# An attention kernel's scan moved to the next step, its hiding to GpSimd, and its narrow counts from ScalarE to VectorE

## The chip, the cores and the metric

The kernel runs on one core of a Trainium2 chip. The metric is the device time of one execution in microseconds (us), the median of three runs. Engines are called by the short names of the profile: PE is TensorE, ACT is ScalarE, DVE is VectorE, POOL is GpSimd, SP issues the transfers.

## The reference

For 16 batches of 512 tokens with 128 channels: `x = x + layernorm(attention(layernorm(x)))`, and then `x = x + layernorm(ffn(layernorm(x)))`. The feed-forward part is gated by silu, with 384 hidden channels. The attention has 16 heads; what matters here is this part of it (shapes for one batch and 16 heads):

```python
dots = jnp.einsum('bhid,bhjd->bhij', q, k) * scale      # 512 x (16 memory + 512) scores
dots = jnp.einsum('bhij,hk->bkij', dots, pre_proj)
dots = jnp.where(causal[None, None], neg, dots)
top = lax.top_k(dots, 64)[0]
vk = top[..., -1:]                                      # the 64th largest of each row
dots = jnp.where(dots < vk, neg, dots)
attn = jax.nn.softmax(dots, axis=-1)
attn = jnp.einsum('bhij,hk->bkij', attn, post_proj)
out = jnp.einsum('bhij,bhjd->bhid', attn, v)
```

## The kernel before

The mixing matrices are folded into the weights ahead of the loop. Then one "step" is one head of one batch; a batch has 16 steps. The 512 rows of a head stand as four tiles of 128 rows. By causality the tiles have 528, 400, 272 and 144 columns (keys and 16 memory columns), 1344 in all. Each engine has its own queue of instructions in the order of the program, and the engines meet at semaphores; `g` is the number of the step over all batches, `s` the step within a batch. The Python branch `lagged(kind, s, lag)` says whether the head that entered `lag` steps ago is worked on in this step.

The 64th largest score of each row is found by guessing a threshold. For a head that entered k+1 steps ago, ACT counts guess k (k = 0, 1, 2): a Sign activation over each tile with the guess as bias, summed by the accumulator (L871). From the counts DVE makes the next guesses with a chain of small instructions on 12 or 24 columns (L1123 to L1149), called the update here; the last of them raises `guess_ready`. After three guesses (LAG_K = 4) DVE counts with the fourth guess and keeps the 0/1 marks in `work` (L1014, "found"), takes the marked scores out of the way (L1080, the hide), scans what is left for its 8 largest (L1092, MAX8, four tiles), and picks the right one of nine by rank (L1099) and value (L1107). POOL computes the rank offsets from the count (L1260). DVE also checks whether the count was near enough (L1078 spread, L1084 missed); PE sums that over the rows (L761, the "FLAG" use of the shared misc banks), ACT copies the sum to `flags` (which raises `misc_free`), and DVE loads it into a register in the next step (L1029). Where it isn't zero an exact search runs, which is rare.

One step later (LAG_P = 5) DVE applies the threshold to the exponentials that ACT made (L1048, four tiles, called the applies) and takes a reciprocal of the sums (L1053). POOL scales by it (L1269) and copies the memory columns out (L1276, pmem). PE transposes the result in three groups (L737), ACT copies each group (L882, probsT), and PE multiplies it into the y bank (L724). In the same step DVE evicts the new head's scores from PSUM (L1061), with its maxima. Layer norms are done by DVE (statistics) and POOL (L1194 to L1210) in certain steps, and the feed-forward part goes through PE, ACT, POOL (L1307) and DVE (L1165) in steps 9 to 14.

The order of DVE in a step before: found, applies, reciprocal, eviction, spread, hide, missed, update, scans, rank, value. The order of ACT: counts of guesses 2 and 1, a copy from misc, the copy for the next head, counts of guess 0, a copy, then probsT copies and exponentials mixed, the flags copy, the last probsT copy. The order of POOL: negated maxima, seed of a guess, offset, scaling, pmem, the memory columns of the new head, extras (norms, gate product). ACT's counts wait for the update of the step before:

```python
at_least(act, first_ready if k == 0 else guess_ready, g if k == 0 else g - 1)
```

and DVE waits for the flags with

```python
dve.wait_ge(misc_free, flag_index(kind, b, s) + 1)   # the FLAG use of step s - 1
```

Of the kernel before, what the change touches and what calls it, by code (L numbers as in the profile page):

```python
# [31 lines left out]
P = 128  # L32
# [9 lines left out]
MASKED = -2.0 ** 100  # L42
# [10 lines left out]
RING = 8  # L53
# [3 lines left out]
LAG_P = 5  # L57
LAG_V = 6
# [18 lines left out]
          4: [("U", 7), ("U", 8)],  # L77
          5: [("PM", 0), ("PM", 1)],
          6: [("U", 9), None],
          7: [("MEM", 0), ("MEM", 1)],  # L80
          8: [("U", 10), ("X1T",)],
          9: [("GATE", 0), ("UP", 0)],
          10: [("GATE", 1), ("UP", 1)],
          11: [("GATE", 2), ("UP", 2)],
          12: [("U", 11), ("U", 12)],
          13: [("DOWN", 0), ("DOWN", 1)],
          14: [("U", 13), ("U", 14)],
          15: [("U", 15), None]}
# [15 lines left out]
def guess_table():  # L104
# [23 lines left out]
    for t in range(T):  # L128
        for i in range(P):
            n = P * t + i + 1  # L130
            z = quantile(min(max((AIM - 0.4 * M) / n, 0.02), 0.97))
            density = n * pdf(z) + M * pdf(z / 4.4) / 4.4
            active = n + M > TOPK
            table[i, t] = z
            table[i, T + t] = z - FAR / (2 * density)
            table[i, 5 * T + 9 * T + t] = float(active)
            table[i, 5 * T + 10 * T + t] = 0.0 if active else -FMAX
        for k in range(GUESSES):
            table[:, 2 * T + k * T + t] = ROW[t] - 2 * AIM - 0.25
        table[:, 5 * T + 9 * t:5 * T + 9 * t + 9] = np.arange(9) - TOPK  # L140
# [8 lines left out]
def flagged(kind, s):  # L149

    return lagged(kind, s, LAG_K)
# [120 lines left out]
def build(nc, table, x, wq, wk, wv, pre, post, memk, memv, wo, bo, wgate, wup, wdown, out):  # L272
    with ExitStack() as ctx:  # L273
# [12 lines left out]
        work = sb("work", [P, WIDE])  # L286
# [37 lines left out]
        onesP = sb("onesP", [P, P])  # L324
        signs = sb("signs", [P, GUESSES, ROW[T - 1]], mybir.dt.int8)
        found = sb("found", [P, T])
# [18 lines left out]
        minus_one = sb("minus_one", [P, T])  # L345
# [72 lines left out]
        found_ready = sem("found_ready")  # L418
        offset_ready = sem("offset_ready")
        select_step = sem("select_step")  # L420
# [140 lines left out]
        def _(pe):  # L561
# [179 lines left out]
            def batch(kind, b, par):  # L741
                def step(s):
# [12 lines left out]
                    if lagged(kind, s, LAG_P):  # L755
                        turn(head_of(s, LAG_P), g - LAG_P, 0)
                        turn(head_of(s, LAG_P), g - LAG_P, 1)
                    if flagged(kind, s):
                        pe.wait_ge(bad_ready, g - LAG_K + 1)
# [3 lines left out]
                    if lagged(kind, s, LAG_P):  # L763
                        turn(head_of(s, LAG_P), g - LAG_P, 2)
# [9 lines left out]
        def _(act):  # L774
# [20 lines left out]
            for q in range(4):  # L795
                nc.scalar.mul(a_all[:, 4 * q:4 * q + 4, :], banks[q][:, :].rearrange("p (h n) -> p h n", h=4),
                              DH ** -0.5).then_inc(a_taken, 1)
            nc.scalar.mul(amem[:, :, :], banks[4][:, 0:H * M].rearrange("p (h n) -> p h n", h=H),
                          DH ** -0.5).then_inc(a_taken, 1)
# [29 lines left out]
            def batch(kind, b, par):  # L829
                def step(s):  # L830
# [30 lines left out]
                    def count(k):  # L861
# [23 lines left out]
                    def exponentials(p):  # L885

                        if lagged(kind, s, LAG_K):
                            ge, t = g - LAG_K, ORDER[p]
# [3 lines left out]
                            nc.scalar.activation(row(expo, ring(head_of(s, LAG_K), ERING), t),  # L892
                                                 row(scores, ring(head_of(s, LAG_K), RING), t), ACT.Exp,
                                                 bias=negmax[:, bass.ds(ring(head_of(s, LAG_K), RING), 1), t]
# [31 lines left out]
        def _(dve):  # L926
# [4 lines left out]
            nc.vector.memset(minus_one[:, :], -1.0).then_inc(consts_made, 1)  # L931
# [35 lines left out]
            nc.vector.tensor_tensor(a_sq[:, :, :], a_all[:, :, :], a_all[:, :, :], ALU.mult).then_inc(squared, 1)  # L967
# [32 lines left out]
            dve.wait_ge(state_set, 3)  # L1000
            nc.vector.tensor_copy(offset[:, :, 9:10].squeeze(2), cap)

            def batch(kind, b, par):
                def step(s):
                    g = b * H + s
                    v = nc.vector
                    slot_k, slot_p = ring(head_of(s, LAG_K), RING), ring(head_of(s, LAG_P), RING)
                    gk, gp = g - LAG_K, g - LAG_P
                    selects, applies = lagged(kind, s, LAG_K), lagged(kind, s, LAG_P)
                    moves = any(lagged(kind, s, k + 1) for k in range(GUESSES))  # L1010
                    now, soon, past = s % STATES, (s + 1) % STATES, (s - 1) % STATES

                    def count_found(t):
                        v.tensor_scalar(work[:, AT[t]:AT[t] + ROW[t]], row(scores, slot_k, t), guessed[:, t:t + 1],  # L1014
                                        None, ALU.is_ge, ALU.add, accum_out=found[:, t:t + 1]).then_inc(found_ready, 1)

                    if selects:
# [6 lines left out]
                        count_found(ORDER[1])  # L1024
                    if applies:

                        dve.wait_ge(misc_free, flag_index(kind, b, s) + 1)
                        alone(dve)
                        rows_missed = dve.value_load(flags[0:1, T:T + 1].bitcast(I32), min_val=0, max_val=2 ** 31 - 1)  # L1029
                    if selects:  # L1030
                        count_found(ORDER[2])
                        count_found(ORDER[3])
                    if applies:

# [19 lines left out]

                    if kind != "drain":
# [9 lines left out]
                    if s == 6 and kind != "first":  # L1065
                        dve.wait_ge(y_taken, b)
                        norm_stats(kind, b, "Y", ybuf)
                    if s == 7 and kind != "first":
# [3 lines left out]
                    if s == 14 and kind != "first":  # L1072
# [3 lines left out]
                    if selects:  # L1076
                        dve.wait_ge(found_ready, 4 * gk + 4)
                        v.scalar_tensor_tensor(out=spread[:, :], in0=found[:, :], scalar=-2.0 * AIM, in1=found[:, :],  # L1078
                                               op0=ALU.add, op1=ALU.mult).then_inc(select_step, 1)
# [3 lines left out]
                        dve.wait_ge(select_step, 1)  # L1083
                        v.scalar_tensor_tensor(out=missed[:, 0:T], in0=spread[:, :], scalar=WINDOW ** 2 + 0.5 - AIM ** 2,  # L1084
                                               in1=active, op0=ALU.is_gt, op1=ALU.mult,
                                               accum_out=missed[:, T:T + 1]).then_inc(bad_ready, 1)

                    def top_scan():
                        if selects:
                            dve.wait_ge(select_step, 2)  # L1090
                            for t in ORDER:
                                v.max(candidates(now)[:, t, 1:9], work[:, AT[t]:AT[t] + ROW[t]]).then_inc(select_step, 1)  # L1092

                    def pick_rank():

                        if selects:
# [249 lines left out]
```

## Time and profile before

| what | value |
|---|---|
| median of three runs | 3636.93 us (3633.64 to 3641.19) |
| the profiled execution: its time | 3636.07 us |
| the profiled execution: its span | 3634.3 us |
| DVE busy | 3292.4 us, 91% of the span |
| ACT busy | 3199.3 us, 88% |
| PE busy | 2795.9 us, 77% |
| POOL busy | 1551.4 us, 43% |

The span runs from the first to the last instruction. Shares are averages over the whole span; what a change is worth is read from one step's order. A row of a timeline has the start in us from the span's start, the duration in us, engine, line, operation, output and input; where an engine stood still before it, the wait and what ended it stand in brackets. Neighbouring DVE or ACT instructions overlap by a little, so a cost in a row of instructions is the distance of starts, not the duration.

### The profile page before, as it was taken

To read this page: it belongs to the slowest core of one execution; us is meant where nothing else is said; L and a number is where in the kernel's file an instruction comes from. 1 tells how busy PE (TensorE), PEld (TensorE's weight loads), DVE (VectorE), ACT (ScalarE), POOL (GpSimd) and SP (SyncE) were. 2 spreads that over 40 slices of the span, in tenths; PEclk is the share of its full clock that TensorE was granted. 3 is DMA by queue.
4 is the path that set the end of the run, shared out by engine and by line. 5 is a ranking of instruction groups with operands and counts; after the bars stand their busy time and mean duration, and the time that the engine had idled before them with its cause. 6 is when DMAs were issued, how large, how long until landed. Compare 5 with 4: busy or idle time off the path is not lost. (4 is left out here: it accounts for less than half of the span.)

```text
span 3634.3 us, 67348 instructions
## 1 busy us (share of the span) xinstructions
PE 2795.9 (77%) x13751; PEld 1808.7 (50%) x13751; DVE 3292.4 (91%) x12492; ACT 3199.3 (88%) x9018; POOL 1551.4 (43%) x2663
## 2 busy tenths in 40 slices
PE   7777778777777878778778867877777788877765
PEld 3455455545545545555455545544555455545544
DVE  4699999999999999999999999999999999999994
ACT  1799999999979999999999979998999999999973
POOL 3233444444434444444444444443444444444433
PEclk9888999988888899888998888899889998899886
DMA  1000000000000000000000000000000000000000
GB/s 41 7 2 2 5 8 5 8 2 5 8 4 8 5 8 2 5 8 5 8 5 7 2 4 8 5 8 2 5 8 5 8 5 8 2 5 8 2 7 4
DMA packets 31375, 22.37 MB, mean 6 GB/s; under 512 B 3201, under 2 KB 30338, under 8 KB 30722
## 3 DMA queue, kind: packets, MB, share of 16 engines
q1 hardware_dynamic: 30722, 16.03, 1.6%
q14 instruction: 532, 4.36, 0.4%
q8 instruction: 121, 1.98, 0.2%
HBM read 11.83 MB, written 4.19 MB: 4 GB/s over the span
## 5 line engine op out<-in xcount | busy, mean ns | idle before, releaser
L871 ACT ACTIVATE signs<-scores,state 128x528 int8<-128x528 f32 (+3 forms) x3072 | 1764.3, 574 | 181.8 <-DVE state L1149 103.4
L713 PE MATMUL s_bank<-xn,gT 128*128 128x512 f32 (+3 forms) x2048 | 900.6, 568 | 1.7 <-issue 0.7
L1269 POOL TENSOR_SCALAR probs<-probs,rinv 128x528 f32<-128x528 f32 (+3 forms) x1024 | 547.1, 553 | 507.3 <-DVE rinv L1053 507.3
L737 PE MATMUL t_bank<-ident,probs 128*128 128x128 f32 x2560 | 482.7, 313 | 299.1 <-POOL probs L1269 289.7
L724 PEld LDWEIGHTS y_bank<-u_all,probsT 128*128 128x128 f32 x5120 | 619.9, 194 | 133.4 <-issue 124.2
L724 PE MATMUL y_bank<-u_all,probsT 128*128 128x128 f32 x5120 | 625.2, 278 | 7.1 <-ACT probsT L882 7.1
L1260 POOL TENSOR_TENSOR offset<-consts,found 128x36 f32<-128x36 f32 x256 | 161.7, 632 | 1047.5 <-DVE work L1014 1047.5
L871 ACT ACTIVATION_READ_ACCUMULATOR signs<-scores,state 128x1 f32 x3072 | 575.7, 187 | 0.0
L737 PEld LDWEIGHTS t_bank<-ident,probs 128*128 128x128 f32 x2560 | 299.7, 153 | 506.8 <-issue 398.6
L1048 DVE SCALAR_TENSOR_TENSOR probs<-scores,kth,expo 128x528 f32<-128x528 f32 (+3 forms) x1024 | 522.8, 565 | 24.8 <-issue 19.1
L892 ACT ACTIVATE expo<-scores,negmax 128x528 f32<-128x528 f32 (+3 forms) x1024 | 535.0, 575 | 0.0
L1014 DVE TENSOR_SCALAR_CACHE_REDUCE work<-scores,state 128x528 f32<-128x528 f32 (+3 forms) x1024 | 515.5, 559 | 20.2 <-issue 12.3
L1061 DVE TENSOR_SCALAR_CACHE_REDUCE scores<-s_bank,memmax 128x512 f32<-128x512 f32 (+3 forms) x1024 | 502.5, 547 | 3.8 <-PE s_bank L715 3.4
L713 PEld LDWEIGHTS s_bank<-xn,gT 128*128 128x128 f32 x2048 | 393.4, 239 | 222.4 <-issue 212.3
L882 ACT COPY probsT<-t_bank 128x512 f32<-128x512 f32 (+1 forms) x768 | 390.6, 509 | 104.5 <-PE t_bank L737 102.7
L1092 DVE MAX8 state<-work 128x8 f32<-128x528 f32 (+3 forms) x1024 | 444.9, 500 | 0.0
L1080 DVE SCALAR_TENSOR_TENSOR work<-work,scores 128x1344 f32<-128x1344 f32 x256 | 404.9, 1582 | 0.0
L599 PE MATMUL misc<-b_all,xn 128*128 128x512 f32 x512 | 281.3, 631 | 50.5 <-ACT u_all L803 46.3
L1276 POOL COPY pmem<-probs 128x64 f32<-128x64 f32 x256 | 303.5, 1186 | 35.9 <-issue 2.5
L761 PE MATMUL misc<-missed,onesP 128*1 128x5 f32 x512 | 49.4, 168 | 343.0 <-DVE missed L1084 340.0
L634 PE MATMUL misc<-xn,a_all 128*128 128x512 f32 x512 | 263.2, 596 | 0.0
L715 PE MATMUL s_bank<-causal,ident 128*128 128x128 bf16 x1024 | 250.5, 245 | 0.0
(148 smaller groups left out, 3384.9 us busy)
## 6 DMA issues: line engine op xcount, KB each, us to landing
xwork<-in_L_attn_x_dram SPq DMA_DIRECT2D x17, 256.0 KB, 2.8
xres<-in_L_attn_x_dram SPq DMA_DIRECT2D x16, 256.0 KB, 2.9
out_dram<-ybuf SPq DMA_DIRECT2D x16, 256.0 KB, 2.4
u_all<-in_L_attn_Wq_dram SPq DMA_DIRECT2D x1, 512.0 KB, 3.7
u_all<-in_L_attn_Wk_dram SPq DMA_DIRECT2D x1, 512.0 KB, 4.5
u_all<-in_L_attn_Wv_dram SPq DMA_DIRECT2D x1, 512.0 KB, 5.3
u_all<-in_L_attn_Wo_dram SPq DMA_DIRECT2D x1, 512.0 KB
expo<-in_L_ffn_w_gate_dram SPq DMA_DIRECT2D x1, 192.0 KB, 4.7
```

The lines of the kernel that those rows point to most:

```text
L713: nc.tensor.matmul(score_part(t, 0, KEYS[t]), lhsT=gT[s % 2][:, t * P:(t + 1) * P], rhs=xn[par][:, 0:KEYS[t]], start=True, stop=False, ski ...
L724: mm = nc.tensor.matmul(y_bank[:, t * P:(t + 1) * P], lhsT=probsT[:, h % 2, at:at + P], rhs=u_all[:, j, h * D:(h + 1) * D], start=False, s ...
L737: mm = nc.tensor.transpose(t_bank[q % 2][:, at:at + P], probs[:, h % 2, KEY_AT[t] + j * P:KEY_AT[t] + (j + 1) * P], ident[:, :])
L871: nc.scalar.activation(signs[:, k, 0:ROW[t]], row(scores, ring(head_of(s, k + 1), RING), t), ACT.Sign, bias=guesses(s % STATES, k, GUESSES ...
L882: nc.scalar.copy(probsT[:, h % 2, PART_AT[q]:PART_AT[q + 1]], t_bank[q % 2][:, 0:PART_AT[q + 1] - PART_AT[q]]).then_inc(t_taken, 1)
L892: nc.scalar.activation(row(expo, ring(head_of(s, LAG_K), ERING), t), row(scores, ring(head_of(s, LAG_K), RING), t), ACT.Exp, bias=negmax[: ...
L1014: v.tensor_scalar(work[:, AT[t]:AT[t] + ROW[t]], row(scores, slot_k, t), guessed[:, t:t + 1], None, ALU.is_ge, ALU.add, accum_out=found[:, ...
L1048: v.scalar_tensor_tensor(out=probs[:, slot_p % 2, AT[t]:AT[t] + ROW[t]], in0=row(scores, slot_p, t), scalar=kth[:, bass.ds(slot_p, 1), t], ...
L1061: v.tensor_scalar(keys(scores, slot, t), score_part(t, 0, KEYS[t]), 1.0, memmax[par][:, t, bass.ds(s, 1)], ALU.mult, ALU.max, accum_out=ro ...
L1080: v.scalar_tensor_tensor(out=work[:, :], in0=work[:, :], scalar=-FMAX, in1=scores[:, bass.ds(slot_k, 1), :].squeeze(1), op0=ALU.mult, op1= ...
L1092: v.max(candidates(now)[:, t, 1:9], work[:, AT[t]:AT[t] + ROW[t]]).then_inc(select_step, 1)
L1269: nc.gpsimd.tensor_scalar(prb, prb, rinv[:, slot_p, t:t + 1], 1.0, ALU.mult, ALU.mult).then_inc(scaled, 1)
```

## The change

1. The scan, rank and value of a head are done one step later and at the start of DVE's step. There are two `work` buffers and two `found` buffers. LAG_P goes from 5 to 6, LAG_V from 6 to 7, and exponentials and flags get a lag of their own, LAG_E = 5. The wait for the flags and their register load stand in front of the third of the four scans.
2. The hide goes from DVE (one instruction, 1344 columns) to POOL (four, one per tile, between its scaling and its pmem copy). Scores are scaled by 2^-60, so that subtracting the 0/1 marks hides a score; MASKED, the guess table and Exp's scale follow.
3. The check (spread, missed) and the update stand behind the value and ahead of found. The update works on the counts of the step before, and writes the guesses for the step that it stands in. Three of the four found counts stand behind the applies.
4. ACT counts three tiles of each guess. DVE counts the 144-wide tile of the three guesses behind the eviction (a compare with accumulation, out to `marks` in bf16), and the update gets one more small instruction for it.
5. POOL's offset and its copy of the memory columns stand at the start of its step; the offset is for the head of LAG_P. ACT's flags copy comes behind the last probsT copy. Extras of PE, the silu product and the norms move by up to one step.

```diff
 LAG_K = 4
-LAG_P = 5
-LAG_V = 6
+LAG_E = 5
+LAG_P = 6
+LAG_V = 7
...
 # ACT, one guess
-                        for p, t in enumerate(ORDER):
+                        for p, t in enumerate(ORDER[:3]):
-                            at_least(act, counted[k], 4 * (g - k - 1) + p)
+                            at_least(act, counted[k], 3 * (g - k - 1) + p)
...
 # ACT, the end of its step
+                    take_turned(2)
                     if flagged(kind, s):
-                        at_least(act, probs_ready, 4 * (g - LAG_K))
+                        at_least(act, probs_ready, 4 * (g - LAG_E))
                         take(kind, b, par, ("FLAG", s), flags[:, :], misc[misc_place(kind, par, ("FLAG", s))][0:1, 0:T + 1])
-                    take_turned(2)
...
 # DVE, the start of its step
+                    if applies:
+                        dve.wait_ge(hidden, 4 * gp + 4)
+                        alone(dve)
+                        for p, t in enumerate(ORDER):
+                            if p == 2:
+                                dve.wait_ge(misc_free, flag_index(kind, b, s) + 1)
+                                alone(dve)
+                                rows_missed = dve.value_load(flags[0:1, T:T + 1].bitcast(I32), min_val=0,
+                                                             max_val=2 ** 31 - 1)
+                            v.max(candidates(past)[:, t, 1:9], work[:, s % 2, AT[t]:AT[t] + ROW[t]]).then_inc(select_step, 1)
+                        dve.wait_ge(offset_ready, gp + 1)
...
 # DVE, behind the rank, the value and the check
+                    if moves:
+                        for k in range(GUESSES):
+                            if lagged(kind, s, k + 2):
+                                dve.wait_ge(counted[k], 3 * (g - k - 1))
+                        guess, other = guesses(last, 0, GUESSES), pair(now, S_OTHER, 1)
+                        dve.wait_ge(narrow_step, sum(lagged(kind, s, k + 2) for k in range(GUESSES)))
+                        dve.sem_clear(narrow_step)
+                        v.scalar_tensor_tensor(out=narrow_miss, in0=narrow[:, :], scalar=-2.0, in1=narrow_aim,
+                                               op0=ALU.mult, op1=ALU.add).then_inc(guess_step, 1)
...
 # DVE, behind the eviction
+                        for k in counts_now:
+                            v.tensor_scalar(marks[:, k], row(scores, ring(head_of(s, k + 1), RING), 0),
+                                            guesses(now, k, GUESSES)[:, 0:1], None, ALU.is_ge, ALU.add,
+                                            accum_out=narrow[:, k:k + 1]).then_inc(narrow_step, 1)
...
-                        v.scalar_tensor_tensor(out=work[:, :], in0=work[:, :], scalar=-FMAX,
-                                               in1=scores[:, bass.ds(slot_k, 1), :].squeeze(1),
-                                               op0=ALU.mult, op1=ALU.add).then_inc(select_step, 1)
...
 # POOL, behind the scaling and ahead of the pmem copy
+                    if lagged(kind, s, LAG_K):
+                        gk, slot_k = g - LAG_K, ring(head_of(s, LAG_K), RING)
+                        for p, t in enumerate(ORDER):
+                            pool.wait_ge(found_ready, 4 * gk + p + 1)
+                            alone(pool)
+                            wrk = work[:, s % 2, AT[t]:AT[t] + ROW[t]]
+                            nc.gpsimd.tensor_tensor(wrk, row(scores, slot_k, t), wrk, ALU.subtract).then_inc(hidden, 1)
```

## Rows read from the trace of the kernel before

**Rows 1.** The page, busy time of each engine

```profile
PE 2795.9 (77%) x13751; PEld 1808.7 (50%) x13751; DVE 3292.4 (91%) x12492; ACT 3199.3 (88%) x9018; POOL 1551.4 (43%) x2663
```

**Rows 2.** Timeline of ACT, the y copies of two neighbouring batches

```profile
1658.25 0.56 ACT L901 COPY ybuf<-y_bank 128x512 f32<-128x512 f32 x1
...
1870.77 0.56 ACT L901 COPY ybuf<-y_bank 128x512 f32<-128x512 f32 x1
```

**Rows 3.** Timeline of DVE over one plain step

```profile
1820.13 0.76 DVE L1014 TENSOR_SCALAR_CACHE_REDUCE work<-scores,state 128x528 f32<-128x528 f32 x1
...
1821.79 0.36 DVE L1014 TENSOR_SCALAR_CACHE_REDUCE work<-scores,state 128x144 f32<-128x144 f32 x1
...
1824.29 0.18 DVE L1053 RECIPROCAL rinv<-rowsum 128x4 f32<-128x4 f32 x1
...
1826.32 0.46 DVE L1078 SCALAR_TENSOR_TENSOR spread<-found 128x4 f32<-128x4 f32 x1
1826.70 1.54 DVE L1080 SCALAR_TENSOR_TENSOR work<-work,scores 128x1344 f32<-128x1344 f32 x1
1828.17 0.19 DVE L1084 SCALAR_TENSOR_TENSOR missed<-spread,consts 128x4 f32<-128x4 f32 x1
...
1828.29 0.25 DVE L1123 TENSOR_TENSOR state<-counts,consts 128x12 f32<-128x12 f32 x1
...
1830.04 0.17 DVE L1149 TENSOR_TENSOR state<-state,move 128x12 f32<-128x12 f32 x1
...
1831.97 0.23 DVE L1099 SCALAR_TENSOR_TENSOR offset<-offset,state 128x36 f32<-128x36 f32 x1
...
1832.63 0.76 DVE L1014 TENSOR_SCALAR_CACHE_REDUCE work<-scores,state 128x528 f32<-128x528 f32 x1
```

**Rows 4.** Timeline of ACT over the same step

```profile
1817.50 0.73 ACT L871 ACTIVATE signs<-scores,state 128x528 int8<-128x528 f32 x1 [0.48 <-DVE state L1149]
...
1819.12 0.52 ACT L871 ACTIVATE signs<-scores,state 128x272 int8<-128x272 f32 x1
...
1819.76 0.41 ACT L871 ACTIVATE signs<-scores,state 128x144 int8<-128x144 f32 x1
...
1820.18 0.72 ACT L871 ACTIVATE signs<-scores,state 128x528 int8<-128x528 f32 x1
...
1829.79 0.36 ACT L882 COPY probsT<-t_bank 128x256 f32<-128x256 f32 x1
```

**Rows 5.** Timeline of ACT in the drain, DVE's register load (line L1029), and the apply behind it

```profile
3580.20 0.14 ACT L803 COPY flags<-misc 1x5 f32<-1x5 f32 x1
...
L1029 DVEq TENSOR_LOAD <-flags x1: 303/303/303, 3580.4 to 3580.4; - x1
...
L1029 DVEq SEQ_ASSERT  x1: 23/23/23, 3581.0 to 3581.0; - x1
...
3581.82 0.77 DVE L1048 SCALAR_TENSOR_TENSOR probs<-scores,kth,expo 128x528 f32<-128x528 f32 x1 [3.33 <-issue]
```

**Rows 6.** Groups of DVE by line and shape

```profile
L1092 DVE MAX8 state<-work 128x8 f32<-128x272 f32 x256 | 110.2, 431 | 0.0
...
L1165 DVE SCALAR_TENSOR_TENSOR f_up<-f_tanh,f_up 128x512 f32<-128x512 f32 x48 | 33.1, 690 | 17.4 <-POOL f_up L1307 15.2 <-issue 2.2
```

**Rows 7.** Timeline of POOL; its 512-wide product; lines L1276, L1260 (ns min/median/max)

```profile
1815.82 0.25 POOL L1194 TENSOR_SCALAR vareps<-meanvar 128x4 f32<-128x4 f32 x1
...
1819.58 0.20 POOL L1249 TENSOR_TENSOR negmax<-rowmax,minus_one 128x4 f32<-128x4 f32 x1
...
1824.66 2.11 POOL L1269 TENSOR_SCALAR probs<-probs,rinv 128x528 f32<-128x528 f32 x4 [1.58 <-DVE rinv L1053]
...
L1307 POOL TENSOR_TENSOR f_up<-f_up,f_gate 128x512 f32<-128x512 f32 x48 | 61.6, 1283 | 8.8 <-ACT f_up L803 8.8
...
L1276 POOL COPY pmem<-probs x256: 236/1441/1455, 156.0 to 3586.5; 128x64 f32<-128x64 f32 x128
...
L1260 POOL TENSOR_TENSOR offset<-consts,found x256: 244/671/811, 136.8 to 3572.5; 128x36 f32<-128x36 f32 x128
```

More of the change, by code:

```diff
@@ L1006, in step @@
                     v = nc.vector
[L1007 to L1011, printed above, removed]
-                    def count_found(t):
-                        v.tensor_scalar(work[:, AT[t]:AT[t] + ROW[t]], row(scores, slot_k, t), guessed[:, t:t + 1],
-                                        None, ALU.is_ge, ALU.add, accum_out=found[:, t:t + 1]).then_inc(found_ready, 1)
+                    slot_k, slot_e, slot_p = [ring(head_of(s, lag), RING) for lag in (LAG_K, LAG_E, LAG_P)]
@@ new lines, in step @@
+                    gk, ge, gp = g - LAG_K, g - LAG_E, g - LAG_P
+                    selects, checks, applies = [lagged(kind, s, lag) for lag in (LAG_K, LAG_E, LAG_P)]
+                    moves = any(lagged(kind, s, k + 2) for k in range(GUESSES))
+                    now, last, past = s % STATES, (s - 1) % STATES, (s - 2) % STATES
+                    def count_found(t):
+                        v.tensor_scalar(work[:, s % 2, AT[t]:AT[t] + ROW[t]], row(scores, slot_k, t), guessed[:, t:t + 1],
+                                        None, ALU.is_ge, ALU.add,
+                                        accum_out=found[:, s % 2, t:t + 1]).then_inc(found_ready, 1)
@@ new lines, in step @@
+                    if checks:
+                        number = found[:, (s - 1) % 2, :]
+                        dve.wait_ge(found_ready, 4 * ge + 4)
+                        alone(dve)
+                        v.scalar_tensor_tensor(out=spread[:, :], in0=number, scalar=-2.0 * AIM, in1=number,
+                                               op0=ALU.add, op1=ALU.mult).then_inc(select_step, 1)
+                        dve.wait_ge(select_step, 1)
+                        v.scalar_tensor_tensor(out=missed[:, 0:T], in0=spread[:, :], scalar=WINDOW ** 2 + 0.5 - AIM ** 2,
+                                               in1=active, op0=ALU.is_gt, op1=ALU.mult,
+                                               accum_out=missed[:, T:T + 1]).then_inc(bad_ready, 1)
@@ L1023, in step @@
                         count_found(ORDER[0])
[L1024 to L1032, printed above, removed]
                     if applies:
@@ L1063, in step @@
                                             accum_out=rowmax[:, bass.ds(slot, 1), t]).then_inc(masked, 1)
-                    if s == 6 and kind != "first":
+                    counts_now = [k for k in range(GUESSES) if lagged(kind, s, k + 1)]
+                    if counts_now:
+                        at_least(dve, first_ready, g if lagged(kind, s, 1) else 0)
+                        at_least(dve, guess_ready, g - 1)
+                        placed = g - s if kind == "drain" else g
+                        dve.wait_ge(mem_placed, placed)
+                        dve.wait_ge(masked, 4 * placed)
+                        alone(dve)
+                        for k in counts_now:
+                            v.tensor_scalar(marks[:, k], row(scores, ring(head_of(s, k + 1), RING), 0),
+                                            guesses(now, k, GUESSES)[:, 0:1], None, ALU.is_ge, ALU.add,
+                                            accum_out=narrow[:, k:k + 1]).then_inc(narrow_step, 1)
@@ L1070, in step @@
                         dve.wait_ge(x1_ready, b)
                         norm_stats(kind, b, "X1", xres)
-                    if s == 14 and kind != "first":
+                    if s == 15 and kind != "first":
                         dve.wait_ge(misc_free, misc_index(kind, b, ("DOWN", 1)) + 1)
                         norm_stats(kind, b, "Z", ybuf)
[L1076 to L1079, printed above, removed]
-                        v.scalar_tensor_tensor(out=work[:, :], in0=work[:, :], scalar=-FMAX,
-                                               in1=scores[:, bass.ds(slot_k, 1), :].squeeze(1),
-                                               op0=ALU.mult, op1=ALU.add).then_inc(select_step, 1)
[L1083 to L1096, printed above, removed]
-                            dve.wait_ge(offset_ready, gk + 1)
-                            dve.wait_ge(select_step, T + 2)
-                            v.scalar_tensor_tensor(out=offset[:, :, 0:9], in0=offset[:, :, 0:9], scalar=0.0,
-                                                   in1=candidates(now), op0=ALU.is_equal,
-                                                   op1=ALU.mult).then_inc(select_step, 1)
```

245 lines of the change are left out of this document (126 added, 119 removed).

## Prediction

> **What bounds the kernel now.** I read the page's first part first: VectorE (DVE) is busy 91% of the span, ScalarE (ACT) 88%, TensorE 77%, GpSimd (POOL) 43% [rows 1]. No transfer matters. Then the timeline of ACT by the copies of the y bank, one per batch: two neighbouring ones are 212.5 us apart, so a head step (16 per batch) takes 13.28 us on the mean [rows 2]. Then the timeline of DVE over one plain step: it starts at 1820.13 and the next at 1832.63, 12.50 us with no real hole [rows 3]; layer norm statistics, the memory maxima and the gating product make the mean 13.28. The timeline of ACT shows nearly the same length of work, with 0.48 us of waiting for the guess update (L1149) at its start [rows 4]. So DVE is the bound and ACT is just under it. What the reader must see is the order: in the step before, the guess update ends at 1817.5 and ACT begins its counts, while DVE begins its next step only at 1820.13. ACT works 2.6 us ahead of DVE, and the flags it copies last are not read before the next DVE step. A trip from one update through ACT's flags to the update that needs them spans two steps, which is why it binds nothing now.
>
> **What leaves and what comes on DVE.** The 1344-wide hide (L1080) goes to POOL: start to start 1.47 us off [rows 3]. The spread before it takes 0.38, held up by POOL; alone about 0.2: 0.18 off. Three 144-wide counts come: one such count lasts 0.36 and overlaps its neighbour, so 0.95 for three, between 0.84 and 1.1 [rows 3]. The extra 3-element miss costs what the missed instruction does, 0.12 [rows 3]. Plain DVE work: 12.50 - 1.47 - 0.18 + 0.95 + 0.12 = 11.92 us. If DVE's own work still set the pace, the change would win 0.58 us a step.
>
> **ACT.** Per step three 144-wide signs go. In a row of four tiles the 272-wide start and the 144-wide start are 0.64 apart and the next guess's first tile comes 0.42 later [rows 4]. The last tile of a guess has no wait behind it (0.41 long, 0.42 to the next), so the 272-wide one, as the last, is followed after its own 0.52: a guess costs 0.54 less, 2.14 in place of 2.68, and the step 1.62 less. From the first count at 1817.50 to the end of the last probsT copy is 12.65 [rows 4]; the flags copy now follows it, its 0.14 [rows 5] overlapping by 0.1. ACT from first count to flags done: 12.65 + 0.04 - 1.62 = 11.07. Steps with one copy fewer and those with the tanh nearly cancel over a batch. Exp's scale and the rescaled constants change no size or count: nothing.
>
> **The order, where the cost is.** The update is moved from the end of a DVE step over the step boundary, behind the scan. In the new code the update in step g writes the guesses that ACT's first count of step g needs (guess_ready is one lower at the same step, and ACT still waits for g-1). ACT's flags copy is still the last thing in step g. DVE in step g+1 waits for it (misc_free) before the third of its four scans, and behind that wait in DVE's queue stand the last scans, rank, value, check, the update, the new applies and the eviction. So the trip closes within one step:
>
> - ACT, first count to flags: 11.07.
> - flags to scan three: in the drain, where DVE waited for them, the flags copy ends at 3580.34, the register load starts at 3580.4 and its assert ends at 3581.0 [rows 5]: 0.7. From both sides: 0.1 if scans are issued past the load, 1.48 if everything waited as the apply there did (it starts at 3581.82, behind a branch as well, which here is after the update). I take 0.7, as the load is the only thing between.
> - two last scans: 0.43 for the 272-wide one [rows 6], 0.3 for the 144-wide one by its columns (an estimate): 0.73.
> - rank, value and the start of what follows: 1831.97 to 1832.63, 0.66 [rows 3].
> - spread 0.2, missed 0.12, extra miss 0.12, update from 1828.29 to 1830.04 + 0.17 = 1.92 [rows 3]: 2.36.
> - update to ACT: 0.03 [rows 3, 4].
>
> Sum 15.55 us, and DVE's 11.92 fit in it with 3.6 us of idling in front of scan three, in which statistics and maxima are covered. TensorE (77% of 13.28, 10.2 us) fits too. No DMA is added; the x load waits for a transposition one step later, far from its use.
>
> **POOL, a second trip.** Its offset is now first in step g+1 but behind everything of step g: rank(g) on DVE to the reciprocal's end 3.02 + first count 0.76 + gap 0.1 + applies 2.08 (half of 1820.13 to 1824.29) + 0.18 = 6.15 [rows 3]; start of the scaling 0.19, scaling 2.11 [rows 7]. The hide: POOL's two-input 512-wide product takes 1.283 and its small ones 0.20 [rows 7], so 2.11 ns an element plus 0.2: 1344 elements in four tiles give 3.64, with a gap 3.77. The pmem copy lasts 0.24 at least and 1.44 in the median; offset 0.24 and 0.67 [rows 7]. The 1.44 ends with DVE's 1344-wide hide, which is gone, and the offset's 0.67 fell into an apply, so I take the low ends: 0.34 and 0.25. Three small ones 0.55. Trip: 13.4; by the medians 15.0. The Trainium skill (SBUF — State Buffer, "SBUF: two separate sides") says that a VectorE instruction with two SBUF inputs and a GpSimd one exclude each other for a whole instruction; the rows agree (0.24 against 1.44), and what DVE now runs beside the hide, counts, eviction and scans, has one SBUF input at most. By it the trip is 13.4.
>
> Plain, this trip is hidden by the 15.55. The extras that POOL does at the end of a step are not: a norm 3.76 + 0.1, with the residual (priced by the 1.28 product) 5.2, twice each per batch; 13.4 + 3.9 = 17.3 and 13.4 + 5.2 = 18.6. Gate products 1.3: 14.7, hidden. DVE's gating product now stands before the update, 0.6 of its 0.69 more in three steps [rows 6].
>
> **Sum.** A batch: 9 x 15.55 + 3 x 16.15 + 2 x 17.3 + 2 x 18.6 = 260.2, against 212.5: +47.7. Times 15 batches: +715, 2 off for the last, which has no x norm. The first batch (ten loaded steps, some 2.3 each) and one more drain step (9), less the rare exact searches that now fall into idling: +30, an estimate. 3634.3 + 743 = 4377 of span, 1.8 around it (3636.07 less 3634.3), and the median of before lies 0.9 higher: about 4380 us.
>
> **Rivals.**
> 1. *The engines' sums decide, the change wins.* If ACT's flags are there when DVE's third scan comes, a step is 0.58 shorter: 16 x 0.58 = 9.3 a batch, about 145 in all: 3490. For it: ACT now has 1.6 less to do and DVE is the bound. Against: the trip would have to be 2.3 us shorter than 15.55 to break even at 13.28, and only 0.6 of it is doubtful. It decides from the point where ACT does not need the update of its own step. 9%.
> 2. *POOL becomes the bound.* If each hide tile waits for the DVE instruction beside it (0.5 to 0.7 each, 2.2 more) and pmem and offset keep their medians, the POOL trip is 15.0 + 2.2 = 17.2 in every step: 16 x 17.2 + 18.2 + 3.9 + 1.8 = 299 a batch, 4960 in all. The busy 43%, two fifths above with the hide, is against it as a sum, not as a trip. 8%. The Trainium skill (Perfetto Trace Analysis, "Optimizing Scalar/DVE Operations") warns that moving work between VectorE and GpSimd might not help, since they share a port; this rival is what that would do here.
> 3. *The stall is covered in part*, so that nothing is won or lost: 3636. It needs a trip of just 13.3. 2%; another 3% for losses between this and my range.
>
> **How the numbers follow.** The trip through ACT has 78%. Its own range: the register load passed by (-0.6 x 255 = -150) gives 4230; POOL's medians add 1.6 in four steps of 15 batches, 96, and 0.25 a step of further waits, 64: 4540. Rival 2 lies above, rival 1 below; leaving both out leaves out about 2 in 10, so the range is 4220 to 4560. A measurement here tells no less than 0.2%, 7 us. Faster 9%, same 2%, slower 89%.
>
> **What will show it.** DVE idle some 3 us before the 272-wide scan in each step, released by ACT's flags; ACT idle about 4 us before its first sign, released by the update; DVE's busy share near 75%, ACT's near 70%; POOL's rank wait visible in four steps of a batch; batch period about 260 us. A hide of 3.6 us on POOL in four tiles; a pmem copy of 0.24. I am wrong if the third scan starts with no wait, if ACT's counts start ahead of the update, or if POOL never idles.

## The result, and the profile after

The changed kernel takes 4384.18 us (median of four runs, 4384.1 to 4385.86) against 3638.12 us for the kernel before (median of four; the 3636.93 of the table above is that of the first three): a ratio of 1.2053, with a 95% interval of 1.2032 to 1.2074. It is 20.5% slower. The forecast was 4380 us, in a range from 4220 to 4560.

The page of the changed kernel, its first line, the busy times and two of the costliest groups:

```profile
span 4382.4 us, 71286 instructions
...
PE 3044.8 (69%) x13751; PEld 2004.1 (46%) x13751; DVE 3024.4 (69%) x14030; ACT 2805.6 (64%) x7482; POOL 1981.4 (45%) x3688
...
L1301 POOL TENSOR_TENSOR work<-scores,work 128x528 f32<-128x528 f32 (+3 forms) x1024 | 887.0, 899 | 13.8 <-DVE work L1020 13.8
...
L1160 DVE TENSOR_SCALAR_CACHE_REDUCE marks<-scores,state 128x144 bf16<-128x144 f32 x768 | 237.0, 358 | 0.0
```

Against [rows 1] DVE's share fell from 91% to 69%, ACT's from 88% to 64%. No engine is near full; the two busy ones are busy for less time (DVE 268 us less, ACT 394 us less) and the span rose by 748. So this is not a price of instructions but of waits. Of DVE's 268 us only about a third is work that left it: the fifteen groups of small instructions from rank to the end of the update that both kernels have fell from 860 to 684 us, and the ones that fell are those that POOL had drawn out (spread 358 ns before and 163 after, product 363 and 183, the last of the update 287 and 171, on the mean). The spread of [rows 3] ends at 1826.78, with POOL's scaling of [rows 7] at 1826.77. The view of waits says between whom (engine and line, us in total, times, longest):

```profile
POOL probs L1293 <- DVE rinv L1135: 2229.7, 256, 24.9
ACT signs L875 <- DVE state L1106: 1298.2, 257, 9.5
DVE state L1034 <- ACT flags L807: 769.8, 252, 5.2
...
DVE offset L1037 <- POOL offset L1283: 123.4, 57, 5.0
```

The second and third row are the two halves of one trip: ACT waits for the update in every step (1298.2 us), and DVE waits for the flags ahead of its third scan in 252 steps (769.8 us). The first row is POOL waiting for DVE; in plain steps that costs nothing, since its offset is still ready ahead of the rank. The last one is the second trip: the rank waits for POOL's offset, 57 times only.

The y copies, one per batch:

```profile
1737.64 0.56 ACT L906 COPY ybuf<-y_bank 128x512 f32<-128x512 f32 x1
...
1998.86 0.56 ACT L906 COPY ybuf<-y_bank 128x512 f32<-128x512 f32 x1
```

261.22 us a batch, against 212.52 [rows 2]. ACT, at the start of a step with a norm and then in one plain step (the bracket is the wait ahead of the instruction, and what ended it):

```profile
2163.33 0.74 ACT L875 ACTIVATE signs<-scores,state 128x528 int8<-128x528 f32 x1 [4.53 <-DVE state L1106]
...
2180.29 0.73 ACT L875 ACTIVATE signs<-scores,state 128x528 int8<-128x528 f32 x1 [5.89 <-DVE state L1106]
...
2190.95 0.36 ACT L886 COPY probsT<-t_bank 128x256 f32<-128x256 f32 x1
2191.20 0.15 ACT L807 COPY flags<-misc 1x5 f32<-1x5 f32 x1
2195.87 0.73 ACT L875 ACTIVATE signs<-scores,state 128x528 int8<-128x528 f32 x1 [4.52 <-DVE state L1106]
```

and DVE in the same plain step (x2 is two scans merged in one row):

```profile
2187.59 1.19 DVE L1034 MAX8 state<-work 128x8 f32<-128x528 f32 x2
2192.08 0.66 DVE L1034 MAX8 state<-work 128x8 f32<-128x272 f32 x2 [3.30 <-ACT flags L807]
2192.85 0.22 DVE L1037 SCALAR_TENSOR_TENSOR offset<-offset,state 128x36 f32<-128x36 f32 x1
2193.21 0.20 DVE L1042 TENSOR_REDUCE kth<-offset 128x4 f32<-128x40 f32 x1
2193.32 0.16 DVE L1049 SCALAR_TENSOR_TENSOR spread<-found 128x4 f32<-128x4 f32 x1
2193.52 0.16 DVE L1052 SCALAR_TENSOR_TENSOR missed<-spread,consts 128x4 f32<-128x4 f32 x1
...
2193.92 0.17 DVE L1078 SCALAR_TENSOR_TENSOR state<-narrow,consts 128x3 f32<-128x3 f32 x1 [0.23 <-remote]
...
2195.66 0.17 DVE L1106 TENSOR_TENSOR state<-state,move 128x12 f32<-128x12 f32 x1
2196.05 0.76 DVE L1020 TENSOR_SCALAR_CACHE_REDUCE work<-scores,state 128x528 f32<-128x528 f32 x1 [0.22 <-DVE state L1106]
```

The reader can walk round the trip here. ACT starts counting at 2180.29; its last probsT copy and then the flags follow, done at 2191.35. DVE had finished two of its scans at 2188.8 and stands still for 3.30 us until the flags are there; the third scan starts at 2192.08. Behind it come the last scan, rank (2192.85), value, spread, the extra miss (2193.92) and the end of the update (2195.66 + 0.17). ACT, idle for 4.52 us, starts its next step at 2195.87, 15.58 us after the last start.

In a step with a norm POOL's trip is the longer one. POOL's timeline, scaling, the hide in four tiles, the pmem copy, the norm from first to last, the offset, and at the end the offset of the plain step above:

```profile
2166.97 2.10 POOL L1293 TENSOR_SCALAR probs<-probs,rinv 128x528 f32<-128x528 f32 x4 [9.44 <-DVE rinv L1135]
2169.04 3.47 POOL L1301 TENSOR_TENSOR work<-scores,work 128x528 f32<-128x528 f32 x4
2172.45 0.24 POOL L1308 COPY pmem<-probs 128x64 f32<-128x64 f32 x1
2172.78 0.24 POOL L1206 TENSOR_SCALAR vareps<-meanvar 128x4 f32<-128x4 f32 x1
...
2175.53 1.04 POOL L1216 TENSOR_TENSOR xwork<-xwork,rstd 128x512 f32<-128x512 f32 x1
...
2176.99 0.24 POOL L1283 TENSOR_TENSOR offset<-consts,found 128x36 f32<-128x36 f32 x1
...
2190.04 0.24 POOL L1283 TENSOR_TENSOR offset<-consts,found 128x36 f32<-128x36 f32 x1
```

and DVE at that time:

```profile
2175.13 0.66 DVE L1034 MAX8 state<-work 128x8 f32<-128x272 f32 x2 [3.29 <-ACT flags L807]
2177.27 0.22 DVE L1037 SCALAR_TENSOR_TENSOR offset<-offset,state 128x36 f32<-128x36 f32 x1 [1.48 <-POOL offset L1283]
```

The third scan waited for the flags, and then the rank waited another 1.48 us for the offset, which POOL could only make behind its norm. In the plain step the offset was ready at 2190.28, 2.57 us before the rank started at 2192.85: POOL's trip alone would have allowed 13.0 us. Beside [rows 7]: the pmem copy takes 0.24, no longer 1.44, since the 1344-wide DVE instruction it used to wait for is gone; and four hide tiles fill the 3.41 us from 2169.04 to the pmem copy.

### The profile page after: what moved, and what is told of

It is laid out like the page before. It is cut to its first block and busy times, and to the rows that moved or that the text cites. A ratio compares the mean times of both kernels' runs of the same rounds, so it can differ in the third digit from the quotient of the medians.

```text
span 4382.4 us, 71286 instructions
## 1 busy us (share of the span) xinstructions
PE 3044.8 (69%) x13751; PEld 2004.1 (46%) x13751; DVE 3024.4 (69%) x14030; ACT 2805.6 (64%) x7482; POOL 1981.4 (45%) x3688
## 5 line engine op out<-in xcount | busy, mean ns | idle before, releaser
L875 ACT ACTIVATE signs<-scores,state 128x528 int8<-128x528 f32 (+2 forms) x2304 | 1445.2, 627 | 1347.9 <-DVE state L1106 1298.2
L1034 DVE MAX8 state<-work 128x8 f32<-128x528 f32 (+3 forms) x1024 | 472.0, 506 | 780.2 <-ACT flags L807 769.8
L1301 POOL TENSOR_TENSOR work<-scores,work 128x528 f32<-128x528 f32 (+3 forms) x1024 | 887.0, 899 | 13.8 <-DVE work L1020 13.8
L719 PE MATMUL s_bank<-xn,gT 128*128 128x512 f32 (+3 forms) x2048 | 857.1, 544 | 6.7 <-ACT gT L807 5.5
L743 PE MATMUL t_bank<-ident,probs 128*128 128x128 f32 x2560 | 588.8, 393 | 317.1 <-POOL probs L1293 192.4
L605 PE MATMUL misc<-b_all,xn 128*128 128x512 f32 x512 | 387.2, 848 | 603.2 <-ACT u_all L807 468.9
L743 PEld LDWEIGHTS t_bank<-ident,probs 128*128 128x128 f32 x2560 | 461.3, 205 | 596.2 <-issue 336.0
L875 ACT ACTIVATION_READ_ACCUMULATOR signs<-scores,state 128x1 f32 x2304 | 432.0, 187 | 0.0
L605 PEld LDWEIGHTS misc<-b_all,xn 128*128 128x128 f32 x512 | 98.2, 240 | 645.4 <-ACT u_all L807 488.5
L1160 DVE TENSOR_SCALAR_CACHE_REDUCE marks<-scores,state 128x144 bf16<-128x144 f32 x768 | 237.0, 358 | 0.0
L699 PE MATMUL misc<-x1T,wgT 128*128 128x512 f32 x96 | 91.7, 1056 | 188.4 <-ACT f_up L807 120.3
```

What stands on the lines that cost most here:

```text
L605: nc.tensor.matmul(misc[misc_place(kind, par, ("U", u))][:, :], lhsT=xn[par][:, (u % 4) * P:(u % 4 + 1) * P], rhs=b_all[:, 4 * (u // 4):4 ...
L719: nc.tensor.matmul(score_part(t, 0, KEYS[t]), lhsT=gT[s % 2][:, t * P:(t + 1) * P], rhs=xn[par][:, 0:KEYS[t]], start=True, stop=False, ski ...
L743: mm = nc.tensor.transpose(t_bank[q % 2][:, at:at + P], probs[:, h % 2, KEY_AT[t] + j * P:KEY_AT[t] + (j + 1) * P], ident[:, :])
L875: nc.scalar.activation(signs[:, k, 0:ROW[t]], row(scores, ring(head_of(s, k + 1), RING), t), ACT.Sign, bias=guesses(s % STATES, k, GUESSES ...
L1034: v.max(candidates(past)[:, t, 1:9], work[:, s % 2, AT[t]:AT[t] + ROW[t]]).then_inc(select_step, 1)
L1301: nc.gpsimd.tensor_tensor(wrk, row(scores, slot_k, t), wrk, ALU.subtract).then_inc(hidden, 1)
```

## The experiments

Four of the ten kernels below start from the changed one and touch one thing; six combine edits. The kernel before ran beside them on the same chip, at about 3636 us each time.

**The flags' wait out of the update's way.** The wait and the load go behind the first found count. `missed` gets two buffers, since the wait had also guarded the one.

```diff
                         for p, t in enumerate(ORDER):
-                            if p == 2:
-                                dve.wait_ge(misc_free, flag_index(kind, b, s) + 1)
-                                alone(dve)
-                                rows_missed = dve.value_load(...)
...
                         count_found(ORDER[0])
                     if applies:
+                        dve.wait_ge(misc_free, flag_index(kind, b, s) + 1)
+                        alone(dve)
+                        rows_missed = dve.value_load(...)
                         dve.wait_ge(exp_ready, 4 * gp + 4)
```

> The flags' wait and register load go behind the first found count, so the update no longer stands behind ACT's flags (missed gets two buffers). Theory (the trip through ACT's flags sets 15.58 us of a plain step): the 3.3 us wait ahead of the third scan goes, the trip spans two steps, and the next bound is POOL's trip through the offset, 13.06 in the changed kernel's trace plus about 0.7 for the load that now stands between rank and reciprocal: 13.8 a plain step, about 245 us a batch, 4130 us. Rival (POOL's trip is already the bound): 4384, no change. Rival (engine sums): no change either, since no work is taken away.

4144.02 us (1.1395, 1.1376 to 1.1414): 240 us off by moving one wait, without a change of work. 4130 was expected. Two neighbouring plain ranks:

```profile
2095.10 0.22 DVE L1032 SCALAR_TENSOR_TENSOR offset<-offset,state 128x36 f32<-128x36 f32 x1 [0.99 <-POOL offset L1282]
2108.87 0.22 DVE L1032 SCALAR_TENSOR_TENSOR offset<-offset,state 128x36 f32<-128x36 f32 x1 [0.98 <-POOL offset L1282]
```

Plain steps take 13.7 to 13.9 us. The trip through ACT's flags was what set 15.58, and POOL's trip is the next thing under it: the rank waits for the offset in 240 of its 256 steps, where it did in 57.

**The offset out of POOL's tail.**

```diff
-                    if lagged(kind, s, LAG_P):
-                        at_least(pool, kth_ready, g - LAG_P)
-                        pool.wait_ge(found_ready, 4 * (g - LAG_P) + 4)
+                    if lagged(kind, s, LAG_E):
+                        at_least(pool, kth_ready, g - LAG_E)
+                        pool.wait_ge(found_ready, 4 * (g - LAG_E) + 4)
...
-                                                found[:, s % 2, :].unsqueeze(2).to_broadcast([P, T, 9]),
+                                                found[:, (s - 1) % 2, :].unsqueeze(2).to_broadcast([P, T, 9]),
```

> POOL makes the offset of the next head ahead of its scaling, in the step before, so that the rank never waits for POOL's hide, pmem copy and norms. Theory: plain steps keep 15.58 (ACT's flags), only the four steps of a batch with a norm fall from 16.96 and 18.3 to about 15.6: 8 us a batch, 4260 us. Rival (POOL's trip is the bound in every step): well over 300 us off. Rival (engine sums): 4384.

4316.09 us (1.1871, 1.1851 to 1.1891). Plain steps keep 15.56 to 15.6, as expected, so POOL's trip does not bind them. The gain is 68 us where 124 were expected: the four norm steps fell to 17.4, 16.2 to 16.3, 17.1 and 16.1, not to 15.6. The trace says what keeps them up. In the one of 17.1, rank to the end of the update takes 4.45 us in place of 2.98: its small instructions are drawn out, as shown with the next experiment (by 0.4 to 0.7 in the others). In the one of 17.4 ACT's part is also longer, 12.55 in place of 11.06, as in the same step of the changed kernel; 0.92 of it is a wait for TensorE. The steps with a gating product stay at 16.0 to 16.4, as they were.

**Both edits.**

> Both edits together. Theory: no trip closes within one step any more, DVE's own work is the bound: 15.58 less the 3.30 of idling is 12.28, and 0.7 of the register load lies open, 13.0 a plain step, 216 us a batch, 3680 us. Rival (a third trip or the TensorE clock, which is granted 0.81 in place of 0.88, takes over): 3900 or more.

3826.7 us (1.0519, 1.0502 to 1.0537), between theory (3680) and rival (3900 or more). Plain steps are 12.9 to 13.1, the 13.0 of the theory. A batch takes 225 to 227 us, not 216. In the step of the Y norm, POOL's timeline, two norm instructions and the residual:

```profile
1759.35 1.04 POOL L1211 TENSOR_TENSOR ybuf<-ybuf,meanvar 128x512 f32<-128x512 f32 x1
1760.53 1.04 POOL L1215 TENSOR_TENSOR ybuf<-ybuf,rstd 128x512 f32<-128x512 f32 x1
1761.71 1.27 POOL L1221 TENSOR_TENSOR xres<-xres,ybuf 128x512 f32<-128x512 f32 x1
```

and DVE's, which are 4-, 24- and 12-column instructions of the check and the update, and the first apply:

```profile
1759.43 0.97 DVE L1047 SCALAR_TENSOR_TENSOR missed<-spread,consts 128x4 f32<-128x4 f32 x1
...
1760.60 1.01 DVE L1080 TENSOR_TENSOR product<-state 128x24 f32<-128x24 f32 x1
...
1761.75 1.25 DVE L1087 SCALAR_TENSOR_TENSOR move<-product,state 128x12 f32<-128x12 f32 x1
...
1766.12 0.77 DVE L1129 SCALAR_TENSOR_TENSOR probs<-scores,kth,expo 128x528 f32<-128x528 f32 x1 [0.99 <-issue]
```

Instructions of 0.16 to 0.18 us last 0.97, 1.01 and 1.25, and each of the long ones ends just as a POOL instruction does (1760.39, 1761.57, 1762.98). They stand until POOL is through. That fits the rule of the Trainium skill that was weighed in the prediction (SBUF — State Buffer, "SBUF: two separate sides"): two SBUF inputs on VectorE and a GpSimd instruction exclude each other. The two instructions with one input in the same stretch bear it out: the value's reduction keeps its 195 ns and the update's reciprocal its 228 ns on the mean in every kernel here. In the changed kernel DVE's waits had kept its check and update clear of POOL's work, and either wait will do: the sixteen groups from rank to the end of the update take 726 us there, 725 in `flags_late` (only the rank's wait left), 769 in `offset_early` (only the flags' wait left) and 893 with both gone. That is 167 us more than in the changed kernel, 10 a batch, which is the missing part. It is also no new cost: without the extra miss the fifteen groups take 836 us, and the kernel before had 860. The last row shows the second cost: 0.99 us of idling ahead of the applies, behind the register load and the branch.

**The load alone.** Only the `value_load` moves; the wait stays ahead of the third scan.

> Only the register load moves behind the first found count; the wait for the flags stays ahead of the third scan. It prices the load within the trip. Theory (load holds the queue for 0.65): plain steps fall to about 14.95, the norm steps grow by some 0.7, since the load now stands between rank and reciprocal: 5 us a batch, 4310 us. Rival (the load is passed by): plain steps keep 15.58 and norm steps grow, 4384 to 4430.

4299.2 us (1.1822, 1.1802 to 1.1841). Two neighbouring third scans:

```profile
2187.83 0.66 DVE L1032 MAX8 state<-work 128x8 f32<-128x272 f32 x2 [1.59 <-ACT flags L807]
...
2202.76 0.66 DVE L1032 MAX8 state<-work 128x8 f32<-128x272 f32 x2 [1.93 <-ACT flags L807]
```

They are 14.93 us apart in place of 15.58: the load takes 0.65 us of the trip. The third scan now starts 0.10 us behind the flags, where it was 0.73. Norm steps grew, as expected.

**The narrow counts back on ACT.** In the changed kernel, the part of the change that the title names is undone.

```diff
-                        for p, t in enumerate(ORDER[:3]):
+                        for p, t in enumerate(ORDER):
...
-                        v.scalar_tensor_tensor(out=narrow_miss, in0=narrow[:, :], scalar=-2.0, in1=narrow_aim,
-                                               op0=ALU.mult, op1=ALU.add).then_inc(guess_step, 1)
-                        v.tensor_tensor(wide_miss, wide_counts, wide_aim, ALU.subtract).then_inc(guess_step, 1)
+                        v.tensor_tensor(miss, counts[:, :], aim_sum, ALU.subtract).then_inc(guess_step, 1)
...
-                        for k in counts_now:
-                            v.tensor_scalar(marks[:, k], row(scores, ring(head_of(s, k + 1), RING), 0), ...)
```

> The narrow counts go back from DVE to ACT, all else stays as changed. Theory (ACT's part of the trip counts in full): ACT grows by 1.62, the update loses the extra miss and its wait, 0.3: 16.9 a plain step, norm steps hardly longer, 15 us a batch, 4630 us, although DVE has 0.95 less to do. Rival (engine sums, with DVE the busiest): faster by up to 0.95 a step, 4140. Rival (POOL's trip): 4384 or 0.3 a step less.

4641.02 us (1.2766, 1.2745 to 1.2787), 257 more. DVE's third scans in two neighbouring plain steps:

```profile
1771.01 0.66 DVE L1034 MAX8 state<-work 128x8 f32<-128x272 f32 x2 [5.72 <-ACT flags L807]
...
1787.92 0.66 DVE L1034 MAX8 state<-work 128x8 f32<-128x272 f32 x2 [5.72 <-ACT flags L807]
```

The expected 4630 holds. DVE, relieved of its narrow counts, only waits longer (5.72 us in place of 3.30), and a plain step takes 16.91 us, the distance of the two. Within this order the narrow counts' move is worth 257 us. It shortens the trip that the rest of the change had closed.

**Opened trips, narrow counts back on ACT.** `both_open` with that edit:

> Both trips opened as in both_open, and the narrow counts back on ACT. Theory: with no trip left the engines' sums decide; DVE 13.0 less 1.25 is 11.75, ACT 11.07 + 1.62 + 0.04 is 12.7 and takes over: about 208 us a batch, 3560 us. If DVE stayed the bound: 195 a batch, 3370. If a trip still ran through ACT within a step: above both_open.

3678.56 us (1.0115, 1.0098 to 1.0132), better than `both_open` by 148 us: with the trips open, the same move has the other sign. The time is above the expected 3560; a batch takes 215.3 to 216.3 in place of 208, again with DVE drawn out: the fifteen groups from rank to update are 196 us busier than in `act_counts_all`, 12 a batch.

**Opened trips, counts covering the load.** All four found counts stand ahead of the applies, the wait and load between the second and third.

> Both trips opened, and all four found counts stand ahead of the applies with the flags' wait and load between the second and the third, so that counts cover the load and the branch. Theory: the 0.7 of the load and the 0.2 ahead of the applies are covered: 12.2 a plain step on DVE, 204 us a batch, 3500 us, faster than the kernel before. Rival (the load wasn't open in both_open): the same as both_open.

3755.39 us (1.0328, 1.0311 to 1.0346): 71 us better than `both_open`, and 255 above what was expected. Plain steps fell by 0.3 to 0.4 only. The rank's group (shapes, busy us, mean ns, idle before):

```profile
L1032 DVE SCALAR_TENSOR_TENSOR offset<-offset,state 128x36 f32<-128x36 f32 x256 | 174.0, 680 | 28.5
```

680 ns in place of 224 in the changed kernel: DVE now reaches the rank while POOL is still in the hide (186 of the 193 ranks that take over 0.4 us run beside it). The time won ahead of the applies is partly lost there. That was not foreseen.

**The same, narrow counts on ACT.** This is the version which the experiments point to.

> both_open_found_first with the narrow counts back on ACT. Its batch of 221 us held some 16 us in which small two-input DVE instructions were drawn out by POOL's. Theory (sums plus this blocking): DVE has 1.28 a step less, 221 - 20 = 201 us a batch; ACT 12.7 a step, 204 a batch, becomes the bound, with DVE longer in norm steps: 209 a batch, 3590 us, some 1.5% faster than the kernel before. Rival (blocking grows as the steps get shorter): 3640 or more.

3620.18 us (0.9956, 0.9942 to 0.9969). It beats the kernel before by 0.4%, little but outside the interval, and the changed one by 764 us. It was expected at 3590 and lies between that and the rival (3640 or more): the rank's mean has grown to 789 ns. The windows of one batch each, with length, busy us and count of PE, PEld, DVE, ACT and POOL in this order, granted clock, DMA share and GB/s: the kernel before, the changed one, `both_open_found_first`, and this one:

```profile
1658.25:1870.77 212.52, 168.43 (x846) 110.15 (x845) 201.24 (x773) 199.09 (x563) 94.96 (x165) 0.89 0.02 6
```

```profile
1737.64:1998.86 261.22, 181.87 (x846) 121.25 (x846) 184.05 (x869) 174.58 (x469) 121.61 (x229) 0.82 0.02 5
```

```profile
1713.69:1934.92 221.23, 174.02 (x860) 115.48 (x858) 200.21 (x870) 174.27 (x469) 123.56 (x229) 0.88 0.02 5
```

```profile
1660.53:1872.72 212.19, 162.36 (x847) 108.87 (x847) 190.48 (x757) 197.24 (x563) 123.77 (x229) 0.93 0.02 6
```

The batch of 212.2 us is the 212.5 of before, with DVE 10.8 us less busy. ACT is the busiest now, at 197 of 212.

**One narrow count of three on DVE.**

> The same, but DVE keeps the narrow count of guess 0 alone, a third of the moved work. Theory: ACT 0.54 a step less, 12.15; DVE 0.6 more (one count, the extra miss, its wait), 210 a batch: 210 to 212 a batch, 3600 us, about the same as with all counts on ACT. If it is clearly the slower of the two, a narrow count costs DVE more than it saves ACT.

3647.59 us (1.0036, 1.0022 to 1.005), 27 us above the version with none, where 10 and "about the same" were expected. A narrow count on DVE brings a count, an extra miss and a wait, and costs more than it saves ACT. That is measured, though its parts were not separated.

**The hide back on DVE, trips open.**

```diff
+                    if selects:
+                        dve.wait_ge(found_ready, 4 * gk + 4)
+                        alone(dve)
+                        v.tensor_tensor(work[:, s % 2, :], scores[:, bass.ds(slot_k, 1), :].squeeze(1), work[:, s % 2, :],
+                                        ALU.subtract).then_inc(hidden, 4)
```

> both_open with the hide back on DVE, behind the narrow counts, one 1344-wide instruction. It prices the hide's move once no trip binds. Theory (DVE's sum): 13.06 + 1.5 = 14.55 a plain step, less a part of the 10 us a batch of blocking: 226 + 24 - 4 = 246 a batch, 4140 us. Rival (POOL's hide costs DVE in blocking what it saves): 226 a batch, 3830.

4125.97 us (1.1348, 1.1331 to 1.1366), 299 above `both_open`. A batch takes 244.1 to 244.7, near the expected 246. So the hide's move to POOL is worth 18 us a batch when the trips are open, its blocking included.

## Why the prediction was right

By its own steps:

- **The order.** Right: the update moved over the step boundary closes a trip through ACT's flags within one step. `flags_late` shows it: the wait moved, no work changed, 240 us off. `load_late` and `act_counts_all` show that the trip's length counts one for one: 0.65 less in it gives 14.93 to 14.95, and 1.3 more gives 16.9, both as forecast.
- **The terms of the plain trip.** ACT 11.07, measured 11.06. Flags to scan three 0.7, measured 0.73. Two scans 0.73, measured 0.77. Rank to spread 0.66, measured 0.47, because the check follows the value more closely than found did. Spread to the end of the update 2.36, measured 2.51, because the extra miss has a wait of its own (0.23 idle, with 0.40 from missed to it, where 0.12 was put). Update to ACT 0.03, measured 0.04. Sum 15.55, measured 15.58; two of the terms were off by 0.15 to 0.2, and cancelled; that the sum fits to 0.03 is luck, that it fits to 0.2 is not.
- **The register load.** The middle value held (0.65 as `load_late` prices it).
- **POOL's trip.** 13.4 forecast. In the step with a norm the trip is 16.96 (ACT's starts at 2163.33 and 2180.29), where 17.3 was forecast; less the 3.9 of the norm, 13.06; the plain step's 15.58 less the 2.57 by which the offset was early gives 13.0 too. The hide was 3.41 where 3.77 was put. The low ends for pmem and offset were right (238 and 246 ns on the mean), so the trip was near 13.4 and not 15.0. That is what the rule of the Trainium skill said that the prediction weighed (SBUF — State Buffer, "SBUF: two separate sides").
- **DVE's own work.** 11.92 was forecast; 15.58 less the 3.30 of waiting is 12.28. The gap is the waits inside the chain (0.23 ahead of the extra miss, 0.22 ahead of found, 0.21 ahead of the applies), not the narrow counts (0.85 for three, 0.95 forecast). Since the load's 0.65 lies within the 3.30, DVE really needs 12.9, which `both_open` shows. It had no weight in the sum, but it would have had in rival 1.
- **Batch and sum.** 260.2 forecast, 260.2 to 261.3 measured in ten batches. The four norm steps of one batch take 18.5, 17.0, 18.3 and 17.6 where two of 17.3 and two of 18.6 were put. The whole came out 4 us off, closer than its terms: between the first and the last but one y copy the batches grew by 661 us, where the forecast of 47.7 each gives 668, and the rest of the run by 87, where it gives 75. One part of the ends' +30 was wrong: the rare exact searches do not fall into idling. The three full batches that hold one take 277.0, 274.7 and 270.0 us, and 229.8, 228.4 and 222.0 before: 8 to 17 us longer than their neighbours in either kernel.
- **The signs.** DVE's wait (3.30), ACT's (4.52), the pmem copy (0.24) and POOL's rank wait came as said. The busy shares came lower: 69% and 64% where 75% and 70% were put.
- **Rival 1**, engines' sums, did not come about: DVE idles ahead of scan three in 252 steps. But its number of 3490 was also wrong as the price of this work with trips open: `both_open` took 3827 and the best arrangement 3620. The forecast looked for blocking between DVE and POOL only beside the hide, and saw that no two-input DVE instruction ran there. That is so only as long as a wait for the flags or for the offset holds the rank back.
- **Rival 2**, POOL as the bound, was wrong for plain steps: `offset_early` left them at 15.58.

What stays open: how the 8 us a batch by which `both_open_act_counts` missed its expectation split between blocking and the order of ACT. No run separates them. Nor does one show what the later scan is worth by itself. Opening the two trips gave 557 of the 746 us back; of what is left, the narrow counts (148) and the register load that lies open (1.0 us in 252 steps of `both_open`) are the parts that were measured.

## What to carry to other kernels

Where several engines run lagged pipelines, follow each datum round the engines back to where it is needed, and count how many steps the trip spans; a trip that closes in one step costs its whole length, however idle the engines are. Moving a block "later" over a step boundary takes a step out of every trip through it: here less work on both busy engines, and still 3.1 us more a plain step (15.58 against 12.50). And a wait can shelter: before removing one, see which instructions would then run beside another engine's and hold each other up.

## What the hardware showed that was not expected

- Small two-input DVE instructions (4 to 24 columns, 0.16 to 0.18 us) stood for up to 1.25 us beside POOL's 512-wide ones of 1.04 and 1.27 us. Over a run the rank alone took 57 us in the changed kernel, 174 in `both_open_found_first` and 202 in the fastest version. Neighbours with one input kept their length.
- The register load holds DVE's queue for 0.65 us, and with the branch behind it some 1 us lies open ahead of the applies when only one count of 0.76 covers it.
- The granted TensorE clock, the mean of a run, was lower where the steps were longer: 0.884 before, 0.808 in the changed kernel, 0.787 with the longest trip, 0.901 in the fastest version. It does not explain the plain step: ACT's 11.06 us hold no wait for TensorE. In one step of some batches ACT does wait for it, by 0.92 us and once by 2.41 in the changed kernel; how much of that is the clock was not measured.
